# Attention scores of a perceiver layer: plain float32 products on four row tiles, with K laid out on the host

## What is computed

```python
# x: 128 batches x 32 rows x 1024;  ctx: 128 x 257 x 256;  all float32
xq = layernorm(x).reshape(b, 32, 8, 4, 32)        # 8 groups, 4 heads per group, 32 features per head
xk = ctx.reshape(b, 257, 8, 32)
scores = einsum('bsgrd,btgd->bgrst', xq, xk) / sqrt(32) + mask
probs  = softmax(scores)
out    = einsum('bgrst,btgd->bsgrd', probs, xk)    # the context is K and V
# then x1 = x + out; S4 convolution of layernorm(x1); 64 experts of rank 8, 16 of them chosen
```

## Time and profile before

| what | before |
|---|---|
| median of the two runs shown | 1293.69 us (1291.55 and 1295.84) |
| span of the profiled execution | 1290.8 us |
| TensorE busy | 1238.7 us, 96% of the span |
| weight loads of TensorE | 1074.4 us, 83%, beside the matmuls |
| ScalarE busy | 1122.5 us, 87% |
| VectorE busy | 1046.6 us, 81% |
| GpSimd busy | 824.7 us, 64% |
| mean granted clock of TensorE | 0.997 |
| transfers | 166 MB in 270,940 packets |

### The profile page before, as it was taken

How to read it: one execution, slowest core, us unless ns; L and a number is a source line. 1 busy time by engine, 2 the same in 40 slices (tenths; PEclk the granted TensorE clock), 3 DMA queues, 4 the chain that set the end, 5 groups by cost and what they waited for, 6 DMA issues and landing times.

```text
span 1290.8 us, 42154 instructions
## 1 busy us (share of the span) xinstructions
PE 1238.7 (96%) x13676; PEld 1074.4 (83%) x13676; DVE 1046.6 (81%) x3552; ACT 1122.5 (87%) x3337; POOL 824.7 (64%) x1259
## 2 busy tenths in 40 slices
PE   4679999999999999999999999999999999999997
PEld 3558888888888888888888888888888888888886
DVE  7978788888888888888888888878888888888753
ACT  5999898998999899899998989998999999898851
POOL 5376666776666677666667766667776666676420
PEclk9899999999999999999999999999999999999999
DMA  8754445554545545454454555445445445554210
GB/s 230 172 133 127 113 128 138 133 143 121 138 127 129 138 123 145 130 140 120 135 138 122 145 131 134 125 121 144 129 123 153 130 116 138 129 140 123 60 59 33
DMA packets 270940, 166.45 MB, mean 129 GB/s; under 512 B 195433, under 2 KB 253298, under 8 KB 270722
## 3 DMA queue, kind: packets, MB, share of 16 engines
q1 hardware_dynamic: 270722, 163.74, 47.5%
HBM read 128.50 MB, written 34.08 MB: 126 GB/s over the span
## 4 chain that ended last, share of the span: by engine, by line
PE 86%; DVE 4%; SPq 3%; issue 2%; DMA 2%; ACT 2%; POOL 1%; DVEq 0%; ACTq 0%; POOLq 0%
PE ps_p L566 25%; PE ps_p L637 16%; PE ps_p L652 15%; PE ps_p L665 14%; PE ps_p L598 9%; PE ps_s L578 8%; SPq L385 2%; DVE ms L1401 1%; DMA dn<-den 1%; ACT pr L853 1%; DVE x L1257 0%; DMA qx<-turn_q 0%; SPq L373 0%; DMA vl<-in_ctx 0%; PE ps_p L524 0%
## 5 line engine op out<-in xcount | busy, mean ns | idle before, releaser
L853 ACT ACTIVATE pr<-ms,negmax 128x256 f32<-128x256 f32 x1024 | 514.7, 505 | 3.8 <-DVE negmax L1401 3.7
L1401 DVE CUSTOM_DVE_ANT_0 ms<-ps_s,neg_mask,last 128x256 f32<-128x256 f32 x1024 | 457.5, 471 | 34.9 <-PE ps_s L578 30.2
L785 ACT ACTIVATE pts<-ps_p 128x512 f32<-128x512 f32 x512 | 295.9, 592 | 48.2 <-PE ps_p L566 44.2
L566 PE MATMUL ps_p<-ident,pr 128*128 128x128 f32 x2048 | 304.8, 277 | 12.0 <-ACT pr L853 4.9
L566 PEld LDWEIGHTS ps_p<-ident,pr 128*128 128x128 f32 x2048 | 238.2, 141 | 49.2 <-issue 16.0
L853 ACT ACTIVATION_READ_ACCUMULATOR pr<-ms,negmax 128x1 f32 x1024 | 200.6, 196 | 0.0
L1075 POOL TENSOR_TENSOR kt<-kr,kt 128x512 fp32r<-128x512 f32 x128 | 165.1, 1290 | 27.9 <-ACT kt L785 27.3
L652 PE MATMUL ps_p<-wa_hi,ut_hi 128*128 128x288 f32 x512 | 177.7, 347 | 1.4 <-DVE ut_lo L1217 1.4
L652 PE MATMUL ps_p<-wa_lo,ut_hi 128*128 128x288 f32 x512 | 151.0, 295 | 0.0
L652 PE MATMUL ps_p<-wa_hi,ut_lo 128*128 128x288 f32 x512 | 150.7, 294 | 0.0
L1117 POOL TENSOR_TENSOR lastp<-lastp 128x256 f32<-128x256 f32 (+4 forms) x320 | 128.7, 402 | 22.6
(11 more groups left out here) (140 smaller groups left out, 2709.6 us busy)
## 6 DMA issues: line engine op xcount, KB each, us to landing
cx<-in_ctx SPq DMA_DIRECT2D x128, 256.0 KB, 3.0
kx<-in_ctx SPq DMA_DIRECT2D x512, 64.0 KB, 2.4
xq<-in_x SPq DMA_DIRECT2D x32, 512.0 KB, 4.2
turn_q<-xq SPq DMA_DIRECT2D x32, 512.0 KB, 3.7
qx<-turn_q SPq DMA_DIRECT2D x128, 128.0 KB, 3.0
xr<-in_x SPq DMA_DIRECT2D x32, 512.0 KB, 4.4
out_x<-tmp SPq DMA_DIRECT2D x32, 512.0 KB, 5.2
dn<-den SPq DMA_DIRECT2D x512, 2.0 KB, 2.0
```

The lines of the kernel that those rows point to most:

```text
L566: mm = pe.transpose(into[:, j * P:(j + 1) * P], source, ident[:, :])
L785: return act.activation(out, in_, ACT.Copy, scale=scale)
L853: act.activation(pr[:, b % 2, g, :], ms[:, n % MS, :], ACT.Exp, bias=negmax[:, n % MS:n % MS + 1], scale=-1.0, accum_out=den[:, b, g:g + 1 ...
L1401: dve.tensor_tensor_reduce(ms[:, n % MS, :], ps_s[:, g % GPH, g // GPH * SW:(g // GPH + 1) * SW], neg_mask[:, 0:SW], 1.0, last[:, it % 2, ...
```

## The change

K is turned on the host: a new input `keys` holds, for each batch, the layout that `kt` needs. One transfer of 256 KB brings it straight into `kt`. `kx`, `kr`, `qs`, and the functions `k_turn`, `k_high`, `k_low`, `q_high` and `q_low` go, with all their calls. `q_turn` writes into `qr`, which now has two buffers by tile. The scores are 2 halves x 4 quarters = 8 matmuls of plain float32 operands in a call. Each list of calls keeps the order of what remains.

```diff
             def load_keys(tile, b):
-                if at(tile, BPT, b - 1) > 0:
-                    sp.wait_ge(kr_done, at(tile, BPT, b - 1))
-                turned = context[tile * BPT + b:tile * BPT + b + 1, 0:2 * P, :].rearrange(
-                    "o (c t) (q e) -> (o t) c q e", t=HEAD_DIM, q=GPH)
-                for quad in range(GPH):
-                    sp.dma_start(kx[HEAD_DIM * quad:HEAD_DIM * (quad + 1), b % 2, :, :, :].rearrange("p c h d -> p c (h d)"),
-                                 turned[:, :, quad, :]).then_inc(kx_loaded[b], 16)
+                if tile > 0:
+                    sp.wait_ge(s_done, at(tile - 1, BPT * GPH, GPH * (b + 1)))
+                sp.dma_start(kt[:, b, :, :].rearrange("p h t -> p (h t)"),
+                             io["keys"][tile * BPT + b:tile * BPT + b + 1, :, :].rearrange("o p c -> (o p) c")).then_inc(kx_loaded[b], 16)
...
             def scores(it, b):
-                pe.wait_ge(kl_done, at(it, BPT, b + 1))
+                pe.wait_ge(kx_loaded[b], at(it, 16, 16))
                 if b == 0:
-                    pe.wait_ge(ql_done, at(it, 2, 2))
+                    pe.wait_ge(qr_done, at(it, 2, 2))
                 pe.wait_ge(ms_done, at(it, STEPS, GROUPS * b))
                 for h in range(HALVES):
-                    for j, (q_part, k_part) in enumerate(((0, 0), (0, 1), (1, 0))):
-                        for quad in range(GPH):
-                            rs = slice(HEAD_DIM * quad, HEAD_DIM * (quad + 1))
-                            mm = pe.matmul(ps_s[:, quad, h * SW:(h + 1) * SW], qs[rs, it % 2, q_part, b, h, :, :].rearrange("p r s -> p (r s)"),
-                                           kt[rs, b, k_part, h, :], start=(j == 0), stop=(j == 2), skip_group_check=True)
-                            if j == 2 and h == HALVES - 1:
-                                mm.then_inc(s_done, 1)
+                    for quad in range(GPH):
+                        rs = slice(HEAD_DIM * quad, HEAD_DIM * (quad + 1))
+                        mm = pe.matmul(ps_s[:, quad, h * SW:(h + 1) * SW], qr[rs, it % 2, h, b, :, :].rearrange("p r s -> p (r s)"),
+                                       kt[rs, b, h, :], start=True, stop=True, skip_group_check=True)
+                        if h == HALVES - 1:
+                            mm.then_inc(s_done, 1)
...
             def q_turn(tile, h):
                 dve.wait_ge(q_moved, at(tile, 64, 64))
-                dve.wait_ge(ql_done, at(tile, 2, h))
-                dve.transpose(qr[:].rearrange("p b r s -> p b (r s)"),
+                if at(tile, BPT * GPH, -BPT * GPH) > 0:
+                    dve.wait_ge(s_done, at(tile, BPT * GPH, -BPT * GPH))
+                dve.transpose(qr[:, tile % 2, h, :, :, :].rearrange("p b r s -> p b (r s)"),
                               qx[:, :, h, :, :].rearrange("p b r d -> p b (r d)")).then_inc(qr_done, 1)
...
-            q_stats(2, 0); maximum(1, 0); weight_low(6, 1); maximum(1, 1); maximum(1, 2); maximum(1, 3)
-            maximum(1, 4); weight_low(7, 0); k_turn(1, 2); maximum(1, 5); maximum(1, 6); maximum(1, 7)
...
+            q_stats(2, 0); maximum(1, 0); weight_low(6, 1); maximum(1, 1); maximum(1, 2); maximum(1, 3); maximum(1, 4)
+            weight_low(7, 0); maximum(1, 5); maximum(1, 6); maximum(1, 7); q_stats(2, 1); q_stats(2, 2); strip_low(0)
...
+    keys = np.asarray(inputs["ctx_1024"])[:, 0:2 * P, :].reshape(BATCHES, 2 * P, GPH, HALVES, HEAD_DIM)
+    return {"x": inputs["x"], "ctx_1024": inputs["ctx_1024"], "keys": keys.transpose(0, 2, 4, 3, 1).reshape(BATCHES, P, 2 * SW), "mask4": np.concatenate([mask] * REP, axis=0),
```

## The result

The changed kernel takes 1311.24 us (median of 1310.21 and 1312.27), the kernel before 1293.69: 1.4% more, ratio 1.014 with a 95% interval from 1.0116 to 1.0165. That is slower beyond doubt, by less than 2%, and 3 us above the forecast of 1308. The profiled execution is the one of 1312.27 us, with a span of 1310.5 us.

What follows compares the result with a forecast made beforehand. TensorE was taken to bound the steady part. From the profiled span, 1290.8 + 20.4 (scores) - 5.0 (head) - 1.0 (stray time) = 1305.2; with the median 2.9 above the span, 1308 us, 1.1% slower, range 1299 to 1320.

Steps and rivals of the forecast that it cites:

- main term: Scores on TensorE: four plain rounds of 0.216 us replace six of 0.1175, 0.159 us more a call, 20.4 us in all.
- the head: Stretch before tile 2's first scores: less ScalarE and VectorE work gains 5.5 us, 5.0 after 0.5 for the clock.
- the stray time: Steady part, tile 2 to 31: of 4.1 us beyond the regular periods, 1 us given back, between 0 and 4.1.
- The bound: Steady part: TensorE sets the pace, busy for all 37.73 us of a period that repeats to a hundredth.
- the relief: Work removed per execution: VectorE 90.1 us, ScalarE 120.1, GpSimd 248.0; counted at nothing in the steady part beside stray time.
- the rival at 1354: Between rounds of a scores call: weight loads no longer hidden, 0.12 us on each of three gaps; chance 0.07.
- the one at 1446: Scores call: two halves of a product block the next product, nine slots, 1.24 us more a call; chance 0.04.
- the one at 1318: Scores call: each pass costs a full float32r round, eight rounds of 0.1175, 0.235 us more; chance 0.08.
- the faster one at 1258: Scores call: row tiles take plain operands at float32r's pace, 0.235 us less a call; chance 0.05.
- about 1314: Whole-kernel time in us that the prediction named if the head ends no earlier than before.
- SyncE's queue: K's loads, one issue instead of four, now wait for the scores of the tile at work; counted at nothing.
- Median and span: Last step of the sum: 2.9 us added to 1305.2, as the median lay that far above the profiled span.

Runs made afterwards that it cites:

- the second set of runs: The changed kernel run again without any edit, four runs: 1313.03 us, ratio 1.0131 to the kernel before.
- Experiment 7: Kernel before with only the first of the three float32r passes of the scores (high parts alone): 1254.24 us, ratio 0.9709.
- experiment 3: Kernel before with plain float32 scores alone; K is still turned and split on the other engines: 1314.54 us, ratio 1.0147.
- experiment 6: Kernel before with a fourth float32r pass added to the scores, low part by low part: 1323.27 us, ratio 1.0243.
- Experiment 4: Kernel before with K turned on the host into three buffers; the high and low split and old scores stay: 1288.59 us, ratio 0.9955.
- the repetitions: Both kernels run and profiled again without edits: the kernel before 1293.98 us, the changed kernel 1313.03 us.
- experiment 5: Changed kernel with the two scores loops exchanged, so a row tile's four instructions follow each other: 1316.06 us, ratio 1.0158.
- experiment 8: Changed kernel with every scores product issued twice, the copy directly after its product: 1433.54 us, ratio 1.1097.
- experiment 9: Changed kernel with every scores product issued twice, the copies after all four row tiles had their first: 1417.73 us, ratio 1.0953.
- experiment 1: The changed kernel again, no edit, four runs: 1313.03 us, ratio 1.0131 to the kernel before.

## Why the prediction was right

The forecast was 1308 us, slower by 1.1%; measured are 1311.24 and, over the second set of runs, a ratio of 1.0131. Its main term was right in mechanism and size. Two small terms, the head and the stray time, were wrong in opposite directions; that the total came within 3 us owes something to luck.

- **The bound.** TensorE sets the pace before and after: the period grew by four times what a call grew (0.68 against 4 x 0.164 = 0.66). Experiment 7 adds how near the next bound lies: about 1.4 us below the period. One reading behind it was too strong: the period of before does not always repeat to a hundredth. 19 of its 28 periods do, the others are up to 39.08 us; in the changed kernel all 28 do.
- **The scores: 0.159 a call forecast, 0.164 measured** (medians of 128 calls: 0.913 and 1.077). Half pace, two instructions for a product, four rounds of 0.216: each is in the rows above. The one composition that the trace of before did not hold, four row tiles with plain operands, behaves as the sum of its two halves. Entry and exit are 0.21 in both kernels (0.913 - 6 x 0.1175, and 1.077 - 4 x 0.2155). Over 128 calls the cost is 21.0 us instead of 20.4; experiment 3, without the relief, moves the medians by 20.1 us, in which the longer period swallows some of the stray time.
- **The weight loads stay hidden.** Rounds 0.2155 apart leave no room for 0.12; the rival at 1354 is refuted. The call of 1.08 us also refutes the rival at 1446, which needs 2.16, and the one at 1318, whose eight rounds take 1.15 (experiment 6 is that call); the faster one at 1258 falls with the half pace.
- **The stray time: 1 us forecast, 3.2 measured** (1098.25 - 28 x 37.73 - 38.60 is 3.2; after, all 28 periods are 38.40 or 38.41, so that nothing is left). The forecast named the right bounds, but had no row that told who caused it. Experiment 4 shows that it goes when K comes turned from the host, at the old period; experiment 3 shows that the longer period swallows it as well. In the full change it is gained once, whichever does it.
- **The head: forecast 3.7 earlier at tile 2 (104.6 to 100.9), measured 0.5 and 1.8** (104.10; 103.34 against 105.10 in the repetitions). This is the step that was mis-sized. In both pairs `cauchy_sums` starts 1.0 us earlier (24.18 against 25.23, 26.04 against 27.00), where 1.6 were forecast. Over all profiles even that is not clear of chance: the five kernels without the relief (before twice, experiments 3, 6, 7) start it at 25.23 to 27.00, and the five with all of it (the changed kernel twice, experiments 5, 8, 9) at 24.18 to 28.88. The rows of TensorE's timeline in the changed kernel that answer to the earlier trace rows:

```profile
24.18 3.59 PE L512 MATMUL ps_p<-x 128*128 128x16 f32 x16 [4.76 <-DVE x L1202]
...
29.49 2.09 PE L565 MATMUL ps_s<-kt,qr 32*128 32x256 f32 x16
```

  In this pair of profiles TensorE's idle time between the first scores and tile 2 fell from 20.0 us to (38.40 - 29.87) + (36.20 - 29.84) = 14.9, just the 5 that were forecast, but tile 2 was not earlier by as much: TensorE was busy for 59.7 us of the stretch instead of 54.1. The eight longer calls explain 1.3 of these 5.6 us at the full clock. The clock can explain most of the rest: it averaged 0.78 in the first tile instead of 0.90, that is (0.22 x 38.40 - 0.10 x 35.80) x 2 = 9.7 us more at the lower of its two levels, 1.2 instead of 2.4 GHz, which is worth up to half of that, 4.9 us, where TensorE is busy (an estimate). The scores calls show it: the four of tile 0 took 2.02 us each, and all eight 12.4 us where they took 9.4 before. The forecast set 0.5 us against this, from the clock of a single execution. But clock alone is not the whole of it. The windows of the first two tiles in the repetitions, before and then after:

```profile
32.30:68.20 35.90, 25.37 (x257) 20.26 (x256) 32.63 (x126) 31.49 (x91) 15.71 (x27) 0.90 0.65 161
68.20:105.10 36.90, 29.68 (x359) 23.05 (x359) 30.61 (x96) 36.28 (x114) 25.83 (x39) 1.00 0.56 147
```

```profile
31.30:65.40 34.10, 23.02 (x226) 17.47 (x225) 29.58 (x120) 29.03 (x88) 8.88 (x21) 0.90 0.58 167
65.40:103.34 37.94, 31.41 (x328) 23.60 (x327) 27.46 (x92) 33.22 (x106) 17.37 (x32) 0.96 0.50 147
```

  The clock is nearly alike, the idle times are too (17.7 and 17.6 us), and tile 2 is 1.8 us earlier. What the relief is worth in the head stays open: between executions tile 2 moves by more than the effect, from 104.61 to 106.77 without the relief (before twice, experiment 3) and from 103.34 to 107.91 with it (the changed kernel twice, experiment 5). The forecast's 5.5 came from the middle of its bounds, for want of a row that said how far ScalarE and VectorE gate the head. The medians of experiments 1 and 3, which differ by all of the relief, are 1.5 us apart. The prediction named about 1314 for a head that ends no earlier, and the four runs of experiment 1 have 1313.03.
- **SyncE's queue: counted at nothing, and right, though it waits more.** The waits of SyncE's queue from 104 to 1254 us (total, times, longest), of the loads of `cx` and of K:

```profile
SPq L355 <- PE ps_p L585: 176.7, 38, 6.2
...
SPq L362 <- PE ps_s L565: 56.0, 53, 1.4
```

  and the same loads before:

```profile
SPq L363 <- PE ps_p L598: 82.0, 30, 4.6
...
SPq L373 <- DVE kr L1408: 15.9, 20, 1.3
```

  The loads of K wait 56.0 us for scores, where the old ones waited 15.9 for VectorE's turns, and the loads of `cx` wait 176.7 where it was 82.0. TensorE has no wait at all in the same stretch, against 2.0 us before; the cover of a whole tile was there.
- **Median and span.** The forecast added 2.9 us to its sum against the span. In every run on record with its span the time is about 1.8 us above it, so the other 1.1 of the 2.9 only says that the profiled execution of before was a shorter one than the median. Its 1305.2 stands against spans of 1310.5 and 1306.3. The tail takes most of the first difference (two products at a lower clock, 3.2 us); against the second, the head (103.34 instead of 100.9) is 2.4 too late and the steady part 1.2 shorter than the 1115.7 that the sum held.

## What to carry to other kernels

Before dropping a split into high and low parts, count a product in passes on the engine that sets the pace: plain float32 is two instructions at half pace here, so it replaces three passes by four, and the work it saves elsewhere counts only where it is late for someone. A cost in the steady part can be read to a few per cent from the distance between starts of rounds, even when two properties are seen in two different places; a gain in the head can't be read from busy times, since clock and transfers there change from one execution to the next (in the two profiles of before, VectorE's first step on `tmp` starts at 11.06 and at 12.74 us; in the second, ScalarE ahead of it waits 3.1 us for the transfer of `tmp`). Where two edits come together, try them apart: here one of them alone (K turned on the host) is 0.45% faster than before, and the other takes 1.5%.

## What the runs showed of the hardware

- Row tiles of the array run at their own pace: with all four instructions of a tile in a row, four tiles still work side by side (call 1.10 us against 1.08). What the order costs there is a small delay at the start of a round: in one round, the four tiles start 3.3 ns apart with one instruction of a tile in a row (before), 6.7 ns with two (the changed kernel) and 13.3 ns with four (experiment 5), that is an estimated 3.3 ns for each instruction that stands in between.
- With two blocks of four in a row (experiment 8) there is a cost of 0.12 us a call that eight rounds in alternating order (experiment 9) do not have.
- The granted clock of the same program falls at other places in each execution, where TensorE has pauses: 0.78 and 0.90 on average in the first tile of the changed kernel and its repetition, and 0.71 or 1.00 in the same stretch of their tails. In the steady part it was 1.00 in every profile. The four runs of experiment 1 spread from 1308.13 us (clock 0.996 over the run) to 1316.26 (0.991), nearly half of what the change itself moves; that the clock makes all of this spread is not shown (another run at 0.996 took 1312.88).
